# Cross-attention in one program: values of two key tiles in one block, with another order of the last query projections and of step 1's rows

## The reference

```
xn  = (x - mean) / sqrt(var + 1e-5) * gamma + beta
Q   = heads(xn @ Wq.T);  K = V = heads(ctx)
P   = softmax(where(mask, Q K^T / sqrt(32), -inf))      # 512 x 1024 for each batch and head
out = x + merge(P V) @ Wout.T
```

## Time and profile before

| | |
|---|---|
| median of 3 runs | 727.6 us (726.88 to 728.45) |
| profiled execution, its own time | 726.73 us |
| its span, first to last instruction | 724.9 us |
| busy: PE, DVE, ACT, POOL | 679.5, 460.0, 339.2, 391.8 us |
| mean granted TensorE clock | 0.976 |
| first score of step 0 | 139.2 us |
| steps 1 to 14 (from the first score behind the row sums in tile 1 to the same one of step 15) | 197.0 to 607.6 us |
| between bias items in the loop | 29.31 us, in two steps 30.25 and 29.93 |
| the last of these, step 14 | 27.9 us |
| start of the output projection | 631.5 us |
| one projection of queries, start to start | 5.4 us |

### The profile page before, as it was taken

How to read it: one execution, slowest core, us unless ns; L and a number is a source line. 1 busy time by engine, 2 the same in 40 slices (tenths; PEclk the granted TensorE clock), 3 DMA queues, 4 the chain that set the end, 5 groups by cost and what they waited for, 6 DMA issues and landing times.

```text
span 724.9 us, 10759 instructions
## 1 busy us (share of the span) xinstructions
PE 679.5 (94%) x3537; PEld 398.5 (55%) x3537; DVE 460.0 (63%) x494; ACT 339.2 (47%) x614; POOL 391.8 (54%) x107
## 2 busy tenths in 40 slices
PE   2789999865999999999999999999999999899998
PEld 2568788633454544444545444444444445578886
DVE  6763333049787786877878868778687676543231
ACT  3741211433566656566666566665666566500000
POOL 1000000045397977968879779797797897910000
PEclk9799999977999999999999999999999999999999
DMA  9621000425245253351542624525335203123231
GB/s 351 175 50 53 30 29 1 109 62 130 56 108 127 64 131 85 79 144 47 129 104 60 156 50 112 127 63 130 78 84 124 67 1 118 58 88 117 86 116 58
DMA packets 40287, 68.10 MB, mean 94 GB/s; under 512 B 5669, under 2 KB 22695, under 8 KB 40239
## 3 DMA queue, kind: packets, MB, share of 16 engines
q1 hardware_dynamic: 40212, 67.64, 34.2%
q10 hardware_dynamic: 36, 0.01, 0.0%
HBM read 25.18 MB, written 4.19 MB: 41 GB/s over the span
## 4 chain that ended last, share of the span: by engine, by line
PE 87%; DVE 4%; ACT 3%; SPq 2%; DMA 2%; issue 2%; POOL 0%; ACTq 0%; DVEq 0%; POOLq 0%
PE MX L910 20%; PE PV L950 17%; PE SX L934 17%; PE MX L1064 12%; PE MX L940 5%; PE PV L873 5%; PE SX L873 5%; PE MX L850 2%; PE MX L920 1%; ACT PR L606 1%; PE SX L865 1%; DMA PR<-in_x 1%; ACT PR L523 1%; DVE QT L723 1%; PE MX L844 1%
## 5 line engine op out<-in xcount | busy, mean ns | idle before, releaser
L728 DVE TENSOR_REDUCE mx<-MX 128x1 f32<-128x1024 f32 x256 | 302.3, 1217 | 114.3 <-PE MX L910 109.7
L606 ACT ACTIVATE PR<-SX 128x512 f32<-128x512 f32 x512 | 268.9, 601 | 179.3 <-PE SX L934 173.7
L484 POOL TENSOR_TENSOR acc<-acc,PR 128x2048 f32<-128x2048 f32 x64 | 293.4, 4585 | 18.1 <-ACT PR L606 12.7
L484 POOL TENSOR_TENSOR acc<-PR 128x2048 f32<-128x2048 f32 x16 | 73.3, 4584 | 226.4 <-ACT PR L606 226.4
L910 PE MATMUL MX<-R 97*128 97x512 f32 x512 | 176.5, 428 | 18.2 <-DVE mx L728 8.4
L934 PE MATMUL SX<-R 99*128 99x512 f32 x512 | 175.8, 420 | 3.7 <-ACT PR L606 3.3
L910 PEld LDWEIGHTS MX<-R 97*128 97x128 f32 x512 | 86.0, 191 | 114.6 <-DVE mx L728 89.2
L950 PE MATMUL PV<-PR,C 128*32 128x512 f32 x1024 | 137.8, 611 | 0.1
L934 PEld LDWEIGHTS SX<-R 99*128 99x128 f32 x512 | 94.5, 191 | 65.7 <-ACT PR L606 36.5
L819 DVE TENSOR_TENSOR PR<-PR,MX 128x512 f32<-128x512 f32 x16 | 10.9, 687 | 53.3 <-PE MX L1064 51.8
L1064 PE MATMUL MX<-R 128*128 128x512 f32 x192 | 44.3, 390 | 0.0
(11 more groups left out here) (82 smaller groups left out, 487.1 us busy)
## 6 DMA issues: line engine op xcount, KB each, us to landing
R<-KTh SPq DMA_DIRECT2D x64, 256.0 KB, 4.3
PR<-in_x SPq DMA_DIRECT2D x16, 512.0 KB, 4.2
C<-in_ctx SPq DMA_DIRECT2D x16, 512.0 KB, 3.4
R<-KTl SPq DMA_DIRECT2D x64, 128.0 KB, 3.9
R<-QT SPq DMA_DIRECT2D x64, 128.0 KB, 2.5
acc<-in_L_xattn_Wq SPq DMA_DIRECT2D x8, 512.0 KB, 3.7
R<-QT SPq DMA_DIRECT2D x64, 64.0 KB, 2.1
C<-in_L_xattn_Wout SPq DMA_DIRECT2D x8, 512.0 KB, 3.3
```

The costliest lines, as they stand in the source:

```text
L484: nc.gpsimd.tensor_tensor(acc[:, :, :], a, PR[:, tt % RING, :, :], ALU.add).then_inc(pool_used, 1)
L606: nc.scalar.activation(PR[:, tt % RING, h, :], SX[(HPG * tt + h) % BANKS][:, :], ACT.Exp, scale=SCALE).then_inc(exp_done, 1)
L728: nc.vector.tensor_reduce(mx[:, u % 2, i:i + 1], MX[par][:, :], mybir.AxisListType.X, ALU.max, negate=True).then_inc(mx_freed, 1)
```

## The change

Values of tiles 1 and 2, 3 and 4, 5 and 6 are issued in pairs at the end of tiles 3, 5 and 7; values(0) stays in tile 1 and values(7) in the next step's tile 0. Each slot of the tables gets a fourth part, `behind`, whose items follow the pair. Some maxima move; the bias item of n + 1 now follows M0 of n + 2. The last projections come in the order (6, 0), (7, 0), (6, 1), (7, 1), and early on (0, 1) comes before (1, 1). Weight buffers change roles, so group 7's weights are in KTh/KTl. The keys of step 1 are transposed after (7, 0), ahead of the bias item of step 0; they are split into KTh_1/KTl_1, in the area of KS[2], and Sync issues their rows ahead of `bias_rows(0, 0)`. Step 1's query rows are issued by ScalarE between its copies of the last two projections. `later_rows(1)` goes ahead of those of steps 2 and 3.

```diff
-W_IN = [1, 0] + [g % 2 for g in range(2, GROUPS)]
+W_IN = [1 - g % 2 for g in range(GROUPS)]
...
-PROJECTED = [0, 2, 3, 1] + list(range(4, STEPS))
+PROJECTED = [0, 2, 1, 3] + list(range(4, STEPS - 4)) + [STEPS - 4, STEPS - 2, STEPS - 3, STEPS - 1]
...
 FIRST_STEP = [
-    ([], [], []),
-    ([], maxima(1, 0), maxima(1, 1)),
-    (maxima(1, 2), maxima(1, 3), keys(2)),
-    (maxima(1, 4), maxima(1, 5), maxima(1, 6)),
-    (maxima(1, 7), maxima(1, 8), maxima(1, 9)),
-    (maxima(1, 10), maxima(1, 11), maxima(1, 12)),
-    (maxima(1, 13), maxima(1, 14), maxima(1, 15)),
-    ([], bias(1) + maxima(2, 0), maxima(2, 1, 2, 3)),
+    ([], [], [], []),
+    ([], maxima(1, 0), maxima(1, 1), []),
+    (maxima(1, 2), maxima(1, 3), keys(2), []),
+    (maxima(1, 4), maxima(1, 5), maxima(1, 6), maxima(1, 7)),
+    ([], maxima(1, 8), maxima(1, 9), []),
+    ([], maxima(1, 10), maxima(1, 11), maxima(1, 12)),
+    ([], maxima(1, 13), maxima(1, 14, 15), []),
+    ([], bias(1) + maxima(2, 0), maxima(2, 1, 2, 3), []),
 ]
 STEP = [
-    ([], maxima(1, 4), keys(2)),
-    ([], sums(-1), maxima(1, 5)),
-    ([], maxima(1, 6), maxima(1, 7)),
-    (maxima(1, 8), maxima(1, 9), maxima(1, 10)),
-    ([], maxima(1, 11), maxima(1, 12)),
-    (maxima(1, 13), maxima(1, 14), maxima(1, 15)),
-    ([], bias(1) + maxima(2, 0), maxima(2, 1)),
-    ([], maxima(2, 2), maxima(2, 3)),
+    ([], maxima(1, 4), keys(2), []),
+    ([], sums(-1), maxima(1, 5), []),
+    ([], maxima(1, 6), maxima(1, 7), []),
+    ([], maxima(1, 8), maxima(1, 9), maxima(1, 10)),
+    ([], maxima(1, 11), maxima(1, 12), []),
+    ([], maxima(1, 13), maxima(1, 14), maxima(1, 15)),
+    ([], maxima(2, 0), bias(1) + maxima(2, 1), []),
+    ([], maxima(2, 2), maxima(2, 3), []),
 ]
...
-              with_group(5, 12, 3), with_group(6, 15, 1), [("bias", 0), ("keys", 1)]]
+              with_group(5, 12, 4), [("wq", GROUPS - 1), ("keys", 1)], [("bias", 0)]]
...
+    KTh_1, KTl_1 = (R[:, at:at + T] for at in (2 * KSZ, 2 * KSZ + T))
...
+            keys_split(1)
+            key_rows(1, KTh_1, KTl_1)
             bias_rows(0, 0)
-
+            sp.wait_ge(rows_in[0], FIRST_ROWS)
             sp.wait_ge(q_done, BATCH * GROUPS - 1)
-            keys_split(1)
-            key_rows(1)
-            queries_split(1)
+            later_rows(1)
             sp.wait_ge(q_done, BATCH * GROUPS)
-            query_rows(1)
-            sp.wait_ge(rows_in[0], FIRST_ROWS)
-            for r in range(1, RING):
+            sp.wait_ge(keys_in, 2 * STACKED)
+            for r in range(2, RING):
                 later_rows(r)
...
-                    key_high(1, BUFFER["keys", 1])
-                for b in range(BATCH):
-                    q_copy(BATCH * g + b, BATCH * g + b)
+                q_copy(BATCH * g, PROJECTED[BATCH * g])
+                if g == GROUPS - 1:
+                    act.wait_ge(qt_lo, 2)
+                    for h in range(HPG):
+                        own = slice(h * HD, (h + 1) * HD)
+                        act.dma_start(QS[1][0:2 * HD, h, :].bitcast(F32), QT[own, :, :].bitcast(F32)).then_inc(queries_in, 16)
+                        act.dma_start(QS[1][2 * HD:3 * HD, h, :].bitcast(F32), QTh[own, :].bitcast(F32)).then_inc(queries_in, 16)
+                q_copy(BATCH * g + 1, PROJECTED[BATCH * g + 1])
+                if g == GROUPS - 2:
+                    act.wait_ge(kt_ready, 2)
+                    nc.scalar.activation(KTh_1, MX[BUFFER["keys", 1]][:, :], ACT.Copy).then_inc(kt_hi, 1)
...
                 if g > 1:
                     pe.wait_ge(q_copied, 2 * g + 1)
-                    project(g, 0)
-                middle = (at + 1 + end + 1) // 2
+                    if g < GROUPS - 1:
+                        project(g, 0)
+                    else:
+                        project(g - 1, 1, bank=0)
+                middle = (at + 1 + end + 1) // 2 if g < GROUPS - 2 else at + 1
...
-                project(g if g > 1 else 0, 1)
+                if g == GROUPS - 2:
+                    pe.wait_ge(wt_lo, GROUPS)
+                    project(g + 1, 0, bank=1)
+                else:
+                    project(g, 1)
...
-                    if tt >= 1:
-                        values(n, u, tt - 1)
-                    elif not first:
+                    if tt == 1:
+                        values(n, u, 0)
+                    elif tt == 0 and not first:
                         values(n - 1, u + RING - 1, TT - 1)
...
                     for item in with_23:
                         mx_item(*item)
+                    if tt >= 3 and tt % 2:
+                        values(n, u, tt - 2)
+                        values(n, u, tt - 1)
+                    for item in behind:
+                        mx_item(*item)
```

More of the change, by code:

```diff
@@ L125, in items_of @@
     if n == STEPS - 2:
-        items[TT - 1] = ([], wout(0), wout(1))
+        items[TT - 1] = ([], wout(0), wout(1), [])
     if n == STEPS - 1:
-        items = [([], [], []) for _ in range(TT)]
+        items = [([], [], [], []) for _ in range(TT)]
         for o, tt in zip(range(2, WOUT_BLOCKS), (1, 2, 3, 5, 6, 7)):
-            items[tt] = ([], sums(-1) if tt == 1 else [], wout(o))
+            items[tt] = ([], sums(-1) if tt == 1 else [], wout(o), [])
     return items
@@ L310, in _, with key_rows @@
             load_values(2, 0, 1)
-            def key_rows(r):
+            def key_rows(r, high=KTh, low=KTl):
                 for h in range(HPG):
@@ L317, in key_rows @@
                     sp.dma_start(KS[r][0:2 * HD, h, :].bitcast(F32),
-                                 KTh[own, :].bitcast(F32).unsqueeze(1).to_broadcast([HD, 2, T])).then_inc(keys_in, 16)
-                    sp.dma_start(KS[r][2 * HD:3 * HD, h, :].bitcast(F32), KTl[own, :].bitcast(F32)).then_inc(keys_in, 16)
+                                 high[own, :].bitcast(F32).unsqueeze(1).to_broadcast([HD, 2, T])).then_inc(keys_in, 16)
+                    sp.dma_start(KS[r][2 * HD:3 * HD, h, :].bitcast(F32), low[own, :].bitcast(F32)).then_inc(keys_in, 16)
             def query_rows(r):
@@ L560, in q_copy @@
                 act.wait_ge(q_done, n + 1)
-                nc.scalar.activation(QA[:, step_of, :], QP[step_of % BATCH][:, :], ACT.Copy).then_inc(q_copied, 1)
+                nc.scalar.activation(QA[:, step_of, :], QP[(step_of if n < 2 * BATCH else n) % 2][:, :], ACT.Copy).then_inc(q_copied, 1)
             def bias_high(n, par):
@@ L588, in _ @@
                     bias_high(0, BUFFER["bias", 0])
-                    act.wait_ge(q_done, BATCH * g)
                     nc.scalar.activation(warm[:, :], cols[:, 0:1], ACT.Exp)
-                    key_high(1, BUFFER["keys", 1])
-                for b in range(BATCH):
-                    q_copy(BATCH * g + b, BATCH * g + b)
+                q_copy(BATCH * g, PROJECTED[BATCH * g])
[9 more added lines that the diff above has]
+                    nc.scalar.activation(KTh_1, MX[BUFFER["keys", 1]][:, :], ACT.Copy).then_inc(kt_hi, 1)
             def exp(n, tt, h):
@@ L626, in step @@
             def step(n, items, at, first=False):
-                for tt, (early, with_01, with_23) in enumerate(items):
+                for tt, (early, with_01, with_23, behind) in enumerate(items):
                     exp(n, tt, 0)
@@ L634, in step @@
                     exp(n, tt, 3)
-                    at = high_and_bias(n, with_23, at)
+                    at = high_and_bias(n, with_23 + behind, at)
                     if isinstance(n, int) and n == STEPS - 1 and tt == TT // 2:
@@ L761, in _ @@
                         maximum(0, 0, item[1], BUFFER[item])
+                    if item[0] == "keys":
+                        dve.wait_ge(kt_hi, 2)
+                        nc.vector.tensor_tensor(KTl_1, MX[BUFFER[item]][:, :], KTh_1.bitcast(F32), ALU.subtract).then_inc(kt_lo, 1)
+                        dve.wait_ge(kt_lo, 2)
+                        dve.sem_inc(mx_freed, 1)
                 if g == GROUPS - 4:
@@ L764, in _ @@
             bias_low(0, BUFFER["bias", 0])
-            key_low(1, BUFFER["keys", 1])
             def wout_parts(o, par):
@@ L866, in transpose_x, with project @@
                 ins.then_inc(xt_ready, 1)
-            def project(g, b, chunks=range(KCH)):
+            def project(g, b, chunks=range(KCH), bank=None):
                 ops = [(WTh, XTh), (WTl, XTh), (WTh, XTl)]
@@ L872, in project @@
                     for o, (w, v) in enumerate(ops):
-                        ins = nc.tensor.matmul(QP[b][:, :], w[W_IN[g]][:, k * P:(k + 1) * P], v[b][:, k, :],
+                        ins = nc.tensor.matmul(QP[b if bank is None else bank][:, :], w[W_IN[g]][:, k * P:(k + 1) * P], v[b][:, k, :],
                                                start=(k == 0 and o == 0), stop=(k == KCH - 1 and o == 2))
@@ L900, in _ @@
                 pe.wait_ge(xt_split, KCH + k + 1)
-                project(1, 1, [k])
+                project(0, 1, [k])
             def max_item(n, u, i, par):
@@ L990, in _ @@
                 before_step_0(at)
```

(7 more changed lines are left out.)

## The result

The changed kernel takes 743.66 us (median of 4, 741.81 to 744.44) against 727.79: ratio 1.0212, 95% interval 1.0193 to 1.0231. It is slower, as forecast; the forecast was 738.7 with a range of 728 to 743, and the time lies 0.7 us above the range.

The account below looks back on a forecast made before the run. TensorE was taken as busy almost without a break in the loop, with short VectorE waits hidden inside. Terms -5.2 + 1.1 + 13.4 + 0.7 + 1.2 = +11.2 on 726.7 gave 737.9, plus 0.9 for the median: 738.7 us, range 728 to 743.

Parts of the forecast that it names:

- the loop's mechanism: Steps 1 to 14: pairs save 1.23 us of TensorE a step but bring some 2.7 of waits for VectorE: +1.03.
- The two waits: Each loop step: TensorE loses 0.83 us at maximum 13 and 0.94 at maximum 1 behind the bias item, awaiting maximum buffers.
- 13.4 + 0.7: Loop term: 13 whole steps cost +13.4 us, and step 14, with fewer waits, +0.7.
- the 2.2 "outside the loop": Rest of the kernel, as summed in the rivals: the change gives 2.2 us there, so small loop changes decide the sign.
- the start-up term: Ahead of step 0: step 1's first maximum comes at 145.7 instead of 150.92, -5.2 us, bounds -3 and -6.
- nearest is their own row, with some of the keys' traffic still ahead of them, so 141.6: Ahead of step 0: the bias rows, queued behind the keys, land at 141.6, range 141.0 to 143.5; all scores wait for them.
- third rival: Start-up: bias rows behind keys, and secondly ScalarE's issuing, cost 4 to 6 us; loop as forecast, 744 (743 to 750), chance 0.08.
- step 0, +1.1: Step 0: the first wait shortens by 1.4, but values moved behind it and VectorE-bound maxima cost more; bounds -1 and +3.
- The hole: Step 0: TensorE still stands while VectorE's cast and subtraction wait for GpSimd's additions; maximum 6 released 18.2 us after step 1's first.
- the bias item comes 0.7 earlier than before: Step 0, behind its long stop: nine remaining maxima run VectorE-bound and the bias item comes 0.7 us earlier.
- the last step: Step 15: savings before a score waiting for ScalarE are wasted and two values items move behind it, +1.2 us, bounds 0.6 and 2.3.
- the case priced at 12.3: Step 15, late score to output projection: 12.3 us if both moved values items run at the low clock, against 10.6 by slots.

Follow-up runs that it names:

- h2: Changed kernel with each VectorE maximum taken over the first 512 of 1024 columns only: 707.83 us, 28.00 us a step.
- e4: Changed kernel with maximum 1 of the next-but-one step moved from behind the bias item to tile 7, maximum 3 behind the last pair: 734.63 us, ratio 1.0107.
- e7: Changed kernel with maximum 1 in tile 7, maximum 3 behind the last pair, second sums transposition after tile 4, no pairs in steps 0 and 15: 718.53 us.
- e2: Changed kernel with the old tables of step 0 and the loop and no pairs, so only the order ahead of step 0 is new: 724.46 us, ratio 0.9964.
- h1: Kernel before the change with each VectorE maximum taken over the first 512 of 1024 columns only: 720.45 us, 28.9 us a step.
- e3: Changed kernel with step 0's two bias DMAs issued ahead of step 1's eight key DMAs in Sync's queue: 743.84 us, ratio 1.0232.
- e9: Changed kernel with all of step 1's rows issued by Sync, bias rows first, and none by ScalarE: 741.53 us, ratio 1.0197.
- e1: Kernel before the change with the new loop table and values in pairs in steps 1 to 14 only: 738.61 us, ratio 1.0156.
- e11: Changed kernel with the keys of step 2 in tile 0 of step 0 instead of tile 2: 732.66 us, ratio 1.0075.

## Why the prediction was right and where it failed

Two terms failed, the one ahead of step 0 and that of step 0 itself; the loop's mechanism was right.

**Right: sign and mechanism of the loop.** The two waits stand where the chain of slots put them, each position within 0.1 us. VectorE as the cause is shown by h2 (the paired kernel gains once reductions are short), e4 (M1's wait goes when the order gives VectorE its 1.95 us) and e7 (M13's goes when the transposition no longer stands ahead of it). The Trainium skill (TensorEngine Tiling (Array Packing), Key Properties) says that a change of tiling mode drains TensorE. The traces agree, with 0.41 us saved for each V that joins another, but this decides the sign only where the waits are gone. The term was 13.4 + 0.7 = 14.1 and is 10.2, 3.9 too much. Of this 2.1 is that steps 1 to 12 take 30.16 and not 30.34. Another 1.6 is that two of them took 0.94 and 0.62 longer than 29.31 before and don't after. Why (they do so in e2 and h1 too, and in no kernel with pairs) stays open. The last 0.2 is in steps 13 and 14: from origin to origin they took 28.87 and 28.37 before, where I had 29.31 and 27.9, and 29.82 and 28.95 after. Two slips did not enter the forecast: two scores stand ahead of M13, as the sum has it, not four; and the 2.2 "outside the loop" holds step 14's +0.7, without which it is 2.9.

**Failed: the start-up term, -5.2, measured -1.0** (-2 by the medians of e2). "nearest is their own row, with some of the keys' traffic still ahead of them, so 141.6" is the step that failed: the first score waited 4.04 us for the bias rows, not 1 to 2, and came at 144.75, past the bound of 143.5. The bias DMAs were issued at 139.48 and 141.04 instead of 138.6 and 139.2, as ScalarE's issues ran at the same time, and the second landed 3.7 us later, near the upper bound of 4.3. Then the third rival's second half, too: ScalarE's copy of the last projection ended at 143.42, hidden behind that. The remaining 1.0 is the low clock in the first scores and V0, which I hadn't priced. The two other orders tried don't mend it: bias first, ScalarE's copy is late (e3); one queue, the fixed rows are (e9). Bias first with ScalarE's copy ahead of its last query DMAs was not tried. The third rival named this place. That its 744 is also the measured time is luck: it had the loop as forecast, which was 3.9 too much, and nothing for the 3.5 that step 0 cost more.

**Failed: step 0, +1.1, measured +4.6.** The hole went as said. The step that failed is "the bias item comes 0.7 earlier than before": it came 0.35 later, 34.82 us after M0 (184.70), as TensorE stood 1.06 us idle ahead of it and 0.40 ahead of M15, waiting for maxima. From the bias item to the origin it was 15.88 us, where 13.5 (11.65 and the 1.85 of V5 and V6) had been forecast. Here the low clock was missing from the term: 184.70 to 192.87 had a mean granted clock of 0.58, M3 at 188.66 takes 1.22, and V5, V6 3.06 instead of 1.85. e9 has the same tables and the same stop ahead of the bias item, 1.07; there the granted clock stays at 1.00, V5 and V6 take 1.86, and the stretch takes 13.73. So 2.1 of the 4.6 are the low clock. Why it fell in one kernel and not in the other stays open; the stop alone does not explain it. e7 and e2 show that the pairs in step 0, with their table, are what costs: without them it takes 45.39 and 45.85.

**Mis-sized: the last step**, +1.2, measured +2.4, just above its upper bound of 2.3. The late score comes as long after the origin as before, 13.9 us, so what the pairs save ahead of it is wasted, as said. Both V3 and V4 then came at the low clock (635.18 to 639.98 at 0.64), the case priced at 12.3 from that score to the output projection; it took 12.47. e1 and e7 give the 23.9 back.

**Sum.** Terms +11.2, measured +16.2: 4.2 + 3.5 - 3.9 + 1.2 = 5.0 apart. The errors partly cancel. The range had been cut at 743 although the third rival alone reached 750.

**The hole of step 0**, which both kernels share, was described rightly but not priced as a thing to remove: e11 takes the ratio from 1.0212 to 1.0075, some 10 us. The Trainium skill (SBUF — State Buffer, Who interferes with whom) says that a VectorE instruction in a two-port mode, which a cast can enter, shares a pair of ports with GpSimd, that one with two SBUF inputs contends with a GpSimd instruction that reads SBUF, and that the later one to issue is blocked until the other ends. The trace agrees: the cast ends 0.2 to 0.3 us behind GpSimd's first addition (half of the 9.20) and the subtraction 0.6 behind the second, and they take 0.43 and 0.69 us where no addition runs (e11). Which mode the cast ran in no run here shows.

## What to carry to other kernels

Removing time from the busiest engine pays only if the engine that feeds or empties its buffers still gets its latency between two uses of one buffer; write that chain down (here 0.67 + 1.22 + 0.06 = 1.95 us with two buffers) before moving anything, and put short items (the bias transposition) where nothing needs its neighbour's buffer. Apply a rearrangement stage by stage: the same pairs cost 5.3 us in step 0 and 2.4 in step 15, while a loop with them is 0.4 a step shorter than before once two waits are gone. When DMAs are moved to a second queue, count the issue time of both queues together.

## What the runs showed that I had not expected

- DMAs took longer to issue where ScalarE and Sync issued side by side: up to 2.59 us on ScalarE and 2.37 on Sync (e3), against 0.6, and 1.07 to 1.72 for every other key row and the first query row, on one queue (e9). The Trainium skill (DMA: Bandwidth & Descriptors, Issuing engines are not separate DMA queues) says that a second issuing engine saves its sequencer's time only; here it saved 2.5 of 15.0 us (e3) and 4.7 of 16.3 (changed kernel).
- A small DMA behind key rows lands 3.7 to 4.4 us after its issue, ahead of them 1.8.
- The same stop of TensorE, 1.06 and 1.07 us behind some 12 us at full clock, was followed by 8 us at 0.58 in the changed kernel (184.70 to 192.87) and by 1.00 throughout in e9 (184.82 to 198.55). Stops of 0.53 and 0.80 in every step of the loop went with 391.80 us at 1.00. So a single trace of such a stop does not price it.
